# Two expert stages of a two-layer transformer kernel: steps of neighbouring chunks moved along VectorE's, ScalarE's and TensorE's order

## The reference, cut to what matters

```python
x = layernorm(x + attention0(x))
# experts of layer 0, E=8, F=256
scores = x @ Wg.T; topk_probs = softmax(top_k(scores, 2))
hidden = silu(x @ W1.T) * (x @ W2.T); expert_out = hidden @ W3.T
x = layernorm(x + sum_e gating[e] * expert_out[e])
# then q, k, v with RoPE for attention 1
x = layernorm(x + attention1(x) + b_out)
# experts of layer 1, E=4, H=512
router_probs = softmax(gelu(x @ rW1 + rb1) @ rW2 + rb2)
yo = gelu(x @ We1[e] + be1[e]) @ We2[e] + be2[e]
x = layernorm(x + sum_e combine_w[e] * yo)
```

## Time and profile before

| | us |
|---|---|
| median of 3 runs | 1613.22 (1602.71 to 2422.7) |
| the profiled execution | 1611.3, its span 1609.5 |
| first experts, from PE's step 1 of chunk 0 to step 1 of chunk 1 | 42.8 |
| six full chunks (1 to 6) of the first experts | 280.2 |
| full attention, about | 591 |
| six full chunks of the last experts, from 1395.5 to 1577.5 | 182.0 |

### The profile page before, as it was taken

One profiled execution on the slowest core, in us unless ns is written; L12 is line 12 of the kernel. 1 busy time (PEld: TensorE's weight loads), 2 busy tenths in 40 slices (PEclk: granted clock), 3 DMA queues, 4 the chain that ended last, 5 costly groups with the idle time before them and its releaser, 6 DMA issues.

```text
span 1609.5 us, 32282 instructions
## 1 busy us (share of the span) xinstructions
PE 1471.5 (91%) x11200; PEld 797.1 (50%) x11200; DVE 1400.4 (87%) x2394; ACT 1202.9 (75%) x1897; POOL 307.5 (19%) x325
## 2 busy tenths in 40 slices
PE   7989898689999999969999999999999998999996
PEld 4333333377777777623333333333333334777775
DVE  5899999878888988887999999999999973788886
ACT  4999999644445454417999999999999986777775
POOL 0000000234455454420000000000000001234333
PEclk9899999799999998966999999999999997999999
DMA  6636432131224431111111111111111110211211
GB/s 203 203 106 182 120 102 86 49 107 40 96 93 127 128 108 66 66 41 51 46 37 37 46 45 38 42 37 36 37 36 36 37 32 28 69 56 63 75 56 40
DMA packets 71026, 116.76 MB, mean 73 GB/s; under 512 B 23808, under 2 KB 33920, under 8 KB 70272
## 3 DMA queue, kind: packets, MB, share of 16 engines
q1 hardware_dynamic: 70912, 115.21, 23.5%
HBM read 73.49 MB, written 41.16 MB: 71 GB/s over the span
## 4 chain that ended last, share of the span: by engine, by line
PE 61%; DVE 15%; ACT 10%; issue 10%; POOL 1%; DMA 1%; DVEq 0%; ACTq 0%; SPq 0%; POOLq 0%
PE full_o L718 14%; PE hid_pair L1031 12%; PE max_pair L689 11%; ACT cprobs L491 7%; PE bank L1134 7%; DVE negmax_h L808 5%; PE score L703 4%; PE causal_o L463 3%; PE triple L447 2%; PE bank L1066 2%; ACT o_sb L779 1%; DVE st L1284 1%; PE hid_pair L952 1%; PE bank L1094 1%; DVE hid_lo L1458 1%
## 5 line engine op out<-in xcount | busy, mean ns | idle before, releaser
L771 ACT ACTIVATE probs<-score 128x512 f32<-128x512 f32 x1024 | 546.6, 596 | 89.5 <-PE score L703 69.5
L808 DVE TENSOR_REDUCE negmax_h<-max_pair 128x2 f32<-128x1024 f32 x512 | 588.6, 1216 | 24.9 <-PE max_pair L689 24.8
L718 PE MATMUL full_o<-probs,v_st 128*32 128x256 f32 x4096 | 337.9, 403 | 17.7 <-ACT o_sb L779 17.7
L703 PE MATMUL score<-q_st,k_st 32*128 32x512 f32 x1024 | 319.9, 510 | 2.6 <-ACT probs L771 2.6
L689 PE MATMUL max_pair<-k_st,q_st 32*128 32x512 f32 x1024 | 264.7, 515 | 12.2 <-DVE negmax_h L808 10.8
L491 ACT ACTIVATE cprobs<-triple 128x1536 f32<-128x1536 f32 x192 | 258.4, 1713 | 5.2 <-PE triple L447 5.2
L689 PEld LDWEIGHTS max_pair<-k_st,q_st 32*128 32x128 f32 x1024 | 97.8, 188 | 236.7 <-DVE negmax_h L808 179.9
L1240 ACT ACTIVATE act_s<-hid_pair 128x512 f32<-128x512 f32 x128 | 76.7, 599 | 149.5 <-PE hid_pair L1031 149.5
L1031 PE MATMUL hid_pair<-x_hi,w_hi 128*128 128x512 f32 x384 | 171.3, 446 | 1.8 <-DVE x_lo L1401 1.0
L521 DVE TENSOR_SCALAR cprobs<-cprobs 128x1536 f32<-128x1536 f32 (+6 forms) x272 | 160.7, 618 | 2.9 <-ACT cprobs L491 2.9
L463 PE MATMUL causal_o<-cprobs,v_st 128*32 128x512 f32 (+3 forms) x1536 | 156.2, 502 | 2.2 <-DVE cprobs L521 2.2
(11 more groups left out here) (157 smaller groups left out, 2001.8 us busy)
## 6 DMA issues: line engine op xcount, KB each, us to landing
gate_all<-gate_scr SPq DMA_DIRECT2D x48, 512.0 KB, 4.3
o_scr<-o_sb SPq DMA_DIRECT2D x64, 256.0 KB, 2.1
k_st<-k_scr SPq DMA_DIRECT2D x64, 128.0 KB, 2.8
q_st<-q_scr SPq DMA_DIRECT2D x128, 64.0 KB, 2.5
k_st<-k_scr SPq DMA_DIRECT2D x64, 96.0 KB
q_st<-q_scr SPq DMA_DIRECT2D x64, 96.0 KB
q_scr<-qk_hi SPq DMA_DIRECT2D x18, 256.0 KB, 4.6
k_scr<-qk_hi SPq DMA_DIRECT2D x18, 256.0 KB, 4.5
```

The costliest lines, as they stand in the source:

```text
L703: nc.tensor.matmul(sbank[L.score_bank(e)][:, :], k_st[p][rows, kt * P:(kt + 1) * P], q_st[p][rows, q0:q0 + w], start=True, stop=True, tile ...
L718: last = nc.tensor.matmul(full_o[SLOT * j:SLOT * (j + 1), cols], v_st[p][:, kt, j, :], probs[s % NP][:, j, cols], start=(kt == 0 and part ...
L771: nc.scalar.activation(probs[s % NP][:, L.HEADS[j], :], sbank[L.score_bank(e)][:, :], ACT.Exp, scale=SCALE).then_inc(L.exp_done, 1)
L808: nc.vector.tensor_reduce(negmax_h[:, qt // TPC, half, heads[0]:heads[1] + 1:2, qt % TPC], ring[slot][:, :, :], AXX, ALU.max, negate=True) ...
```

## The change

Eight numbers of `plan[0]` and four of `plan[1]` move to later steps. In the first experts `norm2` goes from 4 to 6, `x2_turn` 6 to 8, `q` 7 to 9, `k` 8 to 11, `v` 9 to 12, `norm` 3 to 4, `x_turn` 4 to 6, `router` 5 to 7, `weigh` 8 to 10, `g_turn` 10 to 13. In the last experts `x_turn`, `hidden`, `router` and `weigh` each go one step later, and so does `GATES_AT`. The pairs of maxima that the last chunk's back steps carry (`BESIDE_BACK`) move with these steps. ACT's copy of the output comes one step behind `norm2`, and so behind the copies of `x`. The router's wait on `stats2` becomes one on the first link of the back chain (the residual alone). POOL's order follows the new steps.

```diff
-    BESIDE_BACK = {1: (0,), 2: (1,), 4: (2, 3), 7: (4,), 8: (5, 6), 9: (7,)}
+    BESIDE_BACK = {1: (0,), 2: (1,), 6: (2, 3), 9: (4,), 11: (5, 6), 12: (7,)}
...
-        for pl, steps in ((plan[0], (2, 4, 6, 7, 8, 9, 1, 1, 3, 4, None, 5, 8, 10)),
-                          (plan[1], (5, 7, None, None, None, None, 1, 1, 3, 6, 8, 11, 13, None))):
+        for pl, steps in ((plan[0], (2, 6, 8, 9, 11, 12, 1, 1, 4, 6, None, 7, 10, 13)),
+                          (plan[1], (5, 7, None, None, None, None, 1, 1, 3, 7, 9, 12, 14, None))):
             (pl.y_turn, pl.norm2, pl.x2_turn, pl.q, pl.k, pl.v,
              pl.o_turn, pl.o_proj, pl.norm, pl.x_turn, pl.hidden, pl.router, pl.weigh, pl.g_turn) = steps
...
-        GATES_AT, WEIGH_AT = 1, 1
+        GATES_AT, WEIGH_AT = 2, 1
...
-                        pe.wait_ge(st.stats2, back + 1)
+                        pe.wait_ge(st.back_chain, back * BACK_LINKS + 1)
...
-                if layer == 0 and n == pl.norm2:
+                if layer == 0 and n == pl.norm2 + 1:
                     act.wait_ge(st.norm2, back + 1)
...
                 if c > 0:
                     pool_rstd(pool, pc, st.stats2, st.rstd2, 1, c)
+                if c < 2 * B:
+                    pool_add(pool, st, c, 1, 0)
                 if front:
                     pool_x_lower(pool, st, c + 1)
                 if c < 2 * B:
-                    pool_add(pool, st, c, 1, 0)
+                    pool_add(pool, st, c, 2, 0)
                 if front:
                     pool_gate_exp0(pool, st, c + 1)
                 if c < 2 * B:
-                    pool_add(pool, st, c, 2, 0)
+                    pool_add(pool, st, c, 3, 0)
                 if c > 0:
-                    for a in range(2):
-                        pool_rot(pool, st, c - 1, a)
+                    pool_rot(pool, st, c - 1, 0)
                 if c < 2 * B:
-                    pool_add(pool, st, c, 3, 0)
+                    pool_add(pool, st, c, 4, 0)
+                if c > 0:
+                    pool_rot(pool, st, c - 1, 1)
+                if c < 2 * B:
+                    pool_add(pool, st, c, 5, 0)
                 if c > 0:
                     for a in range(2):
                         pool_qk_lower(pool, st, c - 1, a)
-                if c < 2 * B:
-                    pool_add(pool, st, c, 4, 0)
-                    pool_add(pool, st, c, 5, 0)
```

## The result

The changed kernel is slower by a third of a per cent, which is small but outside the interval of no change: median 1612.26 us of 20 runs (1609.35 to 1618.28) against 1607.28 us of 20 for the kernel before, ratio 1.0033 with a 95% interval of 1.0021 to 1.0045. The range held the time, but the sign was wrong: I had forecast a small gain. The median before, over more runs, is 4 us under the profiled execution of 1611.3 from which the sum was made.

The account below looks back on a forecast made before the run. PE's waits, with DVE's work ahead of its top-2 setting x2_turn, were taken to bound the first experts. +5.4 (first experts) - 2.5 (chunk 0) - 6.0 (last experts) = -3.1 on 1611.3 gave 1608.2, taken as 1609; range 1590 to 1624.

Parts of the forecast that it names:

- The exchange of the waits: First experts: old PE waits of 4.0 us replaced by 1.0 at step 4, 3.0 at x2_turn, 0.6 at v.
- the collisions of steps 7, 9 and 13: First experts: DVE's low halves in these steps blocked behind POOL's adds, 0.7 us each.
- signs of being right: First experts: among others, 2.5 to 3.5 us idle before x2_turn and chunks of 46 to 48 us.
- the term of `x_lo`: First experts, step 8: POOL's x_lo might block norm2, top-2 1.3 us later; left out of the sum, rival at 0.20.
- the list of what DVE gets ahead of the top-2: First experts: 16.0 + 2.4 + 0.6 + 0.6 + 1.4 = 21.0 us of DVE work; gate_pre 21.2 us behind step 1.
- the 1.3 of the rival: First experts, step 8: norm2 waiting for x_lo makes top-2 1.3 us later, 48.9 a chunk; chance 0.20.
- chunk 0: First experts' chunk 0: step 4 goes behind the multiplication instead of norm, -2.5 us, from 0 to -4.
- the stretch behind chunk 6: Chunk 7 and the tail keep their order relative to each other: 0.
- The clock's share: First experts: a fall to half clock in each chunk, now where PE is the bound, +1.7 us a chunk.
- Right: the last experts: Last experts: PE's waits 1.7 us instead of 2.6, taken as 1.0 less a chunk, six times: -6.0 us.
- The rival "slower": First experts: norm2 waits for x_lo, 48.9 a chunk, total 1616, or 1620 to 1628; chance 0.20.
- the first case: Main forecast: first experts' chunks 47.6 against 46.7 us, +0.9 each; total 1602 to 1616; chance 0.45.

Follow-up runs that it names:

- rcp_behind: The changed kernel with VectorE's reciprocal one step later, behind the router's top-2 again; 1607.97 us, ratio 1.0008 to before.
- adds_narrow: The changed kernel with POOL's adds of experts 1 and 2 in the first experts on 4 of 512 columns; 1596.40 us, ratio 0.9940 to before.
- xlo_later: The changed kernel with POOL's x_lo behind the add of expert 2 and the gate's power; 1603.24 us, ratio 0.9983 to before.
- copy_behind: The kernel before with only ScalarE's copy of the output to x_tm moved behind the copies of x; 1603.10 us, ratio 0.9984.
- first_only: The kernel before with the change in the first experts alone, last experts as before; 1617.67 us, ratio 1.0067.
- last_only: The kernel before with the change in the last experts alone, first experts as before; 1602.35 us, ratio 0.9965.
- x2_later: The changed kernel with x2_turn at step 9, q at 10, k at 12 and v at 13; 1597.15 us, ratio 0.9941 to before.
- xlo_rcp: The changed kernel with both x_lo and the reciprocal behind the top-2, x2_turn still at step 8; 1596.24 us, ratio 0.9935 to before.
- adds_x_narrow: The changed kernel with POOL's adds of experts 1 and 2, and x_lo from the third chunk on, on 4 of 512 columns; 1587.22 us, ratio 0.9875.
- all_three: The changed kernel with x2_turn, q, k and v one step later, and x_lo and the reciprocal behind the top-2; 1589.69 us, ratio 0.9894.

## Why the prediction was right and wrong

**Right: the mechanism in the first experts.** The exchange of the waits at `x_turn` and the router for one at `x2_turn` is what the trace shows, with the sizes 0.70, 3.88 and 0.42 for the forecast 1.0, 3.0 and 0.6; the reciprocal ahead of the top-2, and the collisions of steps 7, 9 and 13 of 0.7 each, are there. `rcp_behind` (0.4 us of idle time) and `adds_narrow` (1.4) confirm both prices. But the 3.88 us lie above the 2.5 to 3.5 and the chunks of 48.7 above the 46 to 48 that I had named as signs of being right.

**Wrong, first: the term of `x_lo`.** A full chunk grew by 2.0 us (46.7 to 48.7) where I had +0.9. `gate_pre` came 22.05 us behind step 1 and not 21.2; the rest of the list was 0.2 us too long. The step that failed is the list of what DVE gets ahead of the top-2: I had kept `x_lo` out of the sum and as a rival at 0.20, since I saw it beside `norm2` only. It begins 0.1 us ahead of the low half of step 8 and blocks that, by 1.07 us (1.75 - 0.68), the 1.3 of the rival less what overlaps. `xlo_later` takes this away and is 9 us faster than the changed kernel, of which some 6 are the idle time at `x2_turn` (about 2.9 instead of 3.9). The rule that I had cited from the Trainium skill ("SBUF — State Buffer", Who interferes with whom) for `norm2` is shown by a run now too, 2.18 us instead of 1.10 in `adds_narrow`; in the changed kernel the other instruction met it first. I should have asked whether any instruction of that step could be the one blocked, and then the collision would have deserved far more than one chance in five.

**Wrong, second: chunk 0.** Forecast -2.5, measured +1.0. PE left step 4 behind the multiplication, as forecast, but then worked at the lower clock for 5.0 us instead of 3.4 (granted 0.92, against 0.96 in the earlier trace rows), the gates' DMA landed 0.7 us later than in the earlier trace rows, and a new wait of 0.5 for DVE's multiplication stands at step 12. In `adds_narrow`, with a shorter stretch at the lower clock and without that wait, chunk 0 takes 42.0 us, so the -2.5 isn't reached there either. And the stretch behind chunk 6, for which I had 0, costs 0.8.

**The clock's share.** I took 1.7 us for a fall in each chunk, and it costs about 1.6 where PE is the bound. That the falls before were mostly hidden is shown by `copy_behind`: behind `x_turn` a fall adds nothing, since the wait at `x2_turn` shrinks by as much. The sum of a chunk is then 41.3 + 5.0 + 1.6 = 47.9 against 48.7 measured: 0.5 of the difference is PE's own work, 41.8 instead of 41.3, and the rest is chunk 1 (48.8 us), which waits 1.15 us at step 4 instead of 0.7, and chunk 5 (49.5), whose stretch at the lower clock is twice as long as the others' (granted 0.93 against 0.96). Chunk 6 before had lost 2.8 us over the mean of the other five, 46.2, and not the 3.1 over 45.9 that I wrote.

All together the first experts cost 10.3 us by the medians of `first_only`, where I had +2.9. By the two profiles it is 11.7 + 1.0 + 0.8 = 13.5; no run here shows what makes up for the other 3 us.

**Right: the last experts.** -1.0 us a chunk forecast, -1.07 measured (30.35 to 29.28 over five chunks), and -5.1 us for `last_only` against -6.0. The idle times left are 0.27 and 0.53 where I had 0.6 and 0.9, and the wait behind `x_lo` is in one chunk only.

**The baseline.** The sum stood on one profile of 1611.3 us, 4 above the median. The full attention, which the change doesn't touch, took 636.3 us in it and 629.5 after, from its first matmul to the first `o_proj` of the last experts. Windows of that, and of 200 us at its start, before and then after:

```profile
680.90:1317.19 636.29, 599.67 (x5937) 232.69 (x5937) 599.63 (x596) 540.57 (x1021) 31.32 (x93) 0.95 0.14 40
727.00:927.00 200.00, 194.44 (x1920) 73.97 (x1923) 184.95 (x179) 175.59 (x332) 5.79 (x24) 0.93 0.16 45
```

```profile
694.63:1324.14 629.51, 593.97 (x5937) 232.29 (x5937) 598.76 (x596) 540.03 (x1021) 31.48 (x93) 0.96 0.15 43
740.00:940.00 200.00, 193.86 (x1976) 75.77 (x1976) 189.47 (x185) 181.45 (x345) 6.19 (x25) 0.98 0.16 47
```

That is why the two spans differ by 0.8 us and the medians by 5.0: the profile before had lost elsewhere what the change loses in the first experts. Why the attention took longer in it isn't shown; a lower granted clock goes with it. The forecast's absolute 1609 lies near the measured 1612 partly by luck, since the sum started 4 us too high. The rival "slower" at 1616 to 1628 was right in kind: its collision came, with another instruction of DVE as the one blocked, and its threshold of 0.9 us a chunk was passed (48.7 against the 47.6 of the first case). I had given it 0.20.

## What to carry to other kernels

Before spreading steps of a chunk over more time, count what the engine that releases them gets to do in the added time: two steps gave TensorE 4.2 us and VectorE 5.9. Look at what other engines' instructions will start beside it, since each start just ahead of a two-input instruction of VectorE cost 0.7 to 1.1 us here. And idle time of TensorE was cheaper in pieces here: 3.7 us in four pieces of at most 1.4 (`x2_later`) were followed by no fall of the clock, while 3.6 us with 2.45 of it in one piece (`adds_narrow`) were in four chunks of six, and each fall cost 1.6 us more. A fall costs that only where TensorE is what the chunk waits for.

## What the runs showed of the hardware

The fall of the clock went with the idle time ahead of it. In the six full chunks of the kernels with the moved steps it came 6 times behind a longest idle time of 3.9 us (the changed kernel), 5 times at 2.8 to 3.0 (`xlo_later`), 4 times at about 2.5 (`adds_narrow`, `xlo_rcp`), and never where the longest was 1.6 or less (`x2_later`, `adds_x_narrow`, `all_three`). It isn't settled by the idle time alone: chunks of `adds_narrow` with 2.44 and 2.45 us differ, and so do the chunks of `copy_behind`, where it came in 4 of 6 behind about the same idle time at `x_turn` (2.3 to 2.8 us) as in the kernel before, which had 6 of 6. What else decides was not tried.
